# Block 0's attention with two groups of tokens in lockstep, and its weights loaded in two parts

## The chip, the cores and the metric

The kernel runs on one NeuronCore of a Trainium2 chip. Its engines are TensorE (PE: matmuls and transposes, with its own weight loads, PEld), VectorE (DVE), ScalarE (ACT), GpSimd (POOL) and SyncE (SP, which here only issues DMAs). Each engine runs its own instructions in the order in which they were written, and they meet at semaphores. The metric is the device time of one execution in microseconds (us); the figure is the median of several runs.

## The reference

A vision tower: a tokenizer (four Fourier layers) makes 8192 tokens of 64 features, and four blocks, each of an attention part and a feed-forward part, follow. The change touches the attention of block 0 alone. `x` below is the layer-normed `h`, taken as 128 sequences of 64 tokens:

```python
q = x @ Wq + bq
k = x @ Wk + bk
v = x @ Wv + bv
score = jnp.einsum('bnd,bmd->bnm', q, k) / jnp.asarray(d_a, q.dtype)
score = jax.nn.softmax(score, axis=2)
attn = jnp.einsum('bnm,bmd->bnd', score, v)
h = attn @ Wl + bl
mean = jnp.mean(h, axis=(0, 1))
var = jnp.mean((h - mean) ** 2, axis=(0, 1))
y = jax.nn.relu((h - mean) * jax.lax.rsqrt(var + BN_EPS) * gamma + beta)
return y + x
```

The mean and variance at its end run over all 8192 tokens, so that nothing of `y` can be computed before every token has been through the attention.

## The kernel before

The tokenizer (`build_tokenizer`) ends with all its tokens in DRAM, and a barrier. Then comes `build_blocks`. There SP issues the load of all weights (`wts`, 12765 columns of 128 partitions, fp32), of the constants (`cst`), and of the first tokens (`h`), in this order; the other engines wait for the first two on the semaphore `weights_loaded` (`loaded`, 32), and DVE also for the tokens (`h_in`).

The stage `l0a` follows: 8 passes (`ITERS`) over U = 2 units of 512 tokens each. Both units go through one set of tiles: `x_stacked` holds unit 0 and unit 1 side by side, so that one matmul with a block-diagonal weight serves both. One pass is one chain of steps, each on one engine and each waiting for the one before:

- DVE: statistics (L1517), aggregation (L1523), variance plus epsilon (L1541), centring (L1529); POOL: the power of -1/2 (L1547); DVE: scaling into `x_stacked` (L1535)
- PE: transposes, step `x.flip` (L1585); ACT copies them out as `xT_stacked` (L1596)
- PE: `q`, `k`, `v` (L1627; each fp32 matmul stands as two records); ACT evacuates `q` (L1718), DVE `k` (L1729) and `v` (L1731)
- PE: `scores`, 16 matmuls of 64x64; DVE: `max` (L1745) and `diff` (L1748) read them from PSUM; ACT: `exp` (L1720); DVE: sum (L1751), reciprocal (L1753) and product `p` (L1760), and beside the chain `hx` (L1783), which keeps the normed tokens
- PE: transposes `pT` (L1705), ACT copies them (L1722); PE: `attended`, 16 matmuls of 64x64; ACT copies them (L1724); PE: `hl`, a matmul of 512 columns for each unit; DVE: adds the bias into `hl` (L1786)

After pass i has made `hx` of a unit, SP loads that unit's next tokens into the same `h`. After the 8 passes DVE sums `hl` over all tokens (L2823), ACT squares it (L2803), and one long loop of 8 passes runs the stages `l0b` to `l3f`, which are not changed. The order on every engine is that of the code: `l0a_tensor`, `l0a_scalar`, `l0a_vector` and `ln_pool` are each the body of a loop. `need` is a wait on a step's count, and `done` or `done_both` count a step up. PSUM has 8 banks, `B[0][0..3]` and `B[1][0..3]`; a pass uses seven of them.

## Time and profile before

| | us |
|---|---|
| median of 3 runs (lowest to highest) | 8977.72 (8970.33 to 8978.99) |
| the profiled execution | 8975.14 |
| its span, first to last instruction | 8973.3 |
| in it: barrier's end to the first statistics of `l0a` | 21.7 |
| in it: the 8 passes of `l0a` | 209.1 |

The profile gives for each line and engine what was busy and when; "idle before" names what ended a wait. PE was busy for 81% of the span, DVE 64%, ACT 23%, POOL 2%. Those are averages over stages with different limits, so the part that the change touches is read from the timeline and from windows of it. The granted clock (PEclk) is the share of TensorE's full 2.4 GHz: 0.50 is 1.2 GHz.

### The profile page before, as it was taken

The page shows a single profiled execution, that of the slowest core. Times are in us where ns is not written, and L with a number is a line of the kernel's source. Part 1 is how long each engine was busy: PE and PEld are TensorE (multiplying, and loading weights), DVE is VectorE, ACT ScalarE, POOL GpSimd, SP SyncE. Part 2 cuts the span into 40 slices and gives each one's busy share as a digit, 9 for nine tenths or more (in the row PEclk, how much of TensorE's full clock was granted, in tenths as well). Part 3 has the DMA queues.
Part 4 walks back from the last instruction along what each step waited for, and adds up shares of the span by engine and source line. Part 5 has one row for each costly group of instructions (what it writes and reads, how often), then busy time and mean ns, then how long its engine had stood idle before and what let it go on. Part 6 is the DMA issues. An engine that isn't in the chain of part 4 may idle for free. (4 is left out here: it accounts for less than half of the span.)

```text
span 8973.3 us, 126646 instructions
## 1 busy us (share of the span) xinstructions
PE 7286.3 (81%) x40310; PEld 3633.7 (40%) x40310; DVE 5736.5 (64%) x11679; ACT 2020.7 (23%) x3374; POOL 208.5 (2%) x123
## 2 busy tenths in 40 slices
PE   6888886999999799999789999935666666666666
PEld 5544445444444544444442222223333333333333
DVE  4799995788887488888557777734445344454443
ACT  3221212111111211111222222212222322222222
POOL 0000000000000000000000000000000000000000
PEclk8999998999999799999899999957777878777778
DMA  7655557666666766666764444410000000000000
GB/s 216 136 123 122 126 125 205 181 179 179 179 181 176 217 180 179 179 179 179 191 180 117 123 119 120 111 45 1 2 1 2 1 2 2 1 2 2 1 2 2
DMA packets 641710, 957.43 MB, mean 107 GB/s; under 512 B 527640, under 2 KB 531296, under 8 KB 582758
## 3 DMA queue, kind: packets, MB, share of 16 engines
q1 hardware_dynamic: 641416, 953.52, 40.1%
q8 instruction: 183, 3.00, 0.1%
q14 instruction: 111, 0.91, 0.0%
HBM read 621.96 MB, written 344.28 MB: 108 GB/s over the span
## 5 line engine op out<-in xcount | busy, mean ns | idle before, releaser
L603 PE MATMUL abank<-inv_basis,mode_tile 128*128 128x512 f32 x2048 | 1019.5, 622 | 172.8 <-DMA mode_tile<-m_modes 164.0
L970 DVE TENSOR_TENSOR work<-inv_copy,abank 128x512 f32<-128x512 f32 x1024 | 657.4, 683 | 610.7 <-ACT inv_copy L845 610.2
L665 PEld LDWEIGHTS gbank<-fwd_basis,turned 128*128 128x128 f32 x6368 | 747.2, 193 | 369.7 <-issue 222.7
L665 PE MATMUL gbank<-fwd_basis,turned 128*128 128x128 f32 x6368 | 823.0, 283 | 51.3 <-ACT turned L853 51.3
L1001 DVE TENSOR_TENSOR arena<-zbank,work 128x512 f32<-128x512 f32 x1024 | 701.6, 685 | 208.0 <-PE zbank L638 207.9
L634 PE MATMUL zbank<-arena,conv_bd 128*64 128x512 f32 x3072 | 830.3, 619 | 3.0 <-DVE mixed L1159 2.2
L636 PE MATMUL zbank<-arena,conv_bd 128*64 128x504 f32 x3072 | 779.6, 586 | 0.0
L638 PE MATMUL zbank<-arena,conv_bd 128*64 128x504 f32 x3072 | 779.6, 586 | 0.0
L1003 DVE SCALAR_TENSOR_TENSOR arena<-arena 128x512 f32<-128x512 f32 x1024 | 708.5, 692 | 35.4
L853 ACT ACTIVATE turned<-tbank 128x512 f32<-128x512 f32 x796 | 432.0, 594 | 1100.7 <-PE tbank L652 1100.7
L603 PEld LDWEIGHTS abank<-inv_basis,mode_tile 128*128 128x128 f32 x2048 | 364.3, 196 | 540.1 <-issue 496.9
L652 PEld LDWEIGHTS tbank<-eye,work 128*128 128x128 f32 x3184 | 344.2, 141 | 367.8 <-issue 278.9
L652 PE MATMUL tbank<-eye,work 128*128 128x128 f32 x3184 | 437.6, 281 | 51.1 <-DVE work L1027 34.5
L845 ACT ACTIVATE inv_copy<-abank,conv_bias 128x512 f32<-128x512 f32 x256 | 176.0, 688 | 1237.5 <-PE abank L603 1237.5
L1585 PE MATMUL banks<-constants,x_stacked 128*128 128x128 f32 x256 | 69.5, 426 | 446.9 <-DVE x_stacked L1535 446.9
L802 PE MATMUL zbank<-mix_w,arena 128*128 128x128 f32 x1024 | 243.2, 414 | 208.1 <-DVE mix_w L1149 130.0
L1149 DVE SCALAR_TENSOR_TENSOR mix_w<-uv,twid,partial 128x512 f32<-128x512 f32 x256 | 181.1, 749 | 351.8 <-ACT partial L930 343.5
L636 PEld LDWEIGHTS zbank<-arena,conv_bd 128*64 128x64 f32 x3072 | 220.8, 137 | 440.2 <-issue 440.2
L638 PEld LDWEIGHTS zbank<-arena,conv_bd 128*64 128x64 f32 x3072 | 220.5, 137 | 428.4 <-issue 428.4
L845 ACT ACTIVATE inv_copy<-abank 128x512 f32<-128x512 f32 x256 | 152.9, 597 | 1060.1 <-PE abank L603 1060.1
L1627 PE MATMUL banks<-xT_stacked,weights 64*128 64x512 f32 (+1 forms) x912 | 347.3, 804 | 50.2 <-ACT xT_stacked L1596 37.9
L981 DVE TENSOR_TENSOR work<-work 128x512 f32<-128x512 f32 x512 | 352.3, 688 | 20.9
(306 smaller groups left out, 9251.8 us busy)
## 6 DMA issues: line engine op xcount, KB each, us to landing
h_rows<-arena SPq DMA_DIRECT2D x192, 1024.0 KB, 16.2
arena<-h_rows SPq DMA_DIRECT2D x192, 1024.0 KB, 6.1
arena<-h_rows SPq DMA_DIRECT2D x384, 496.0 KB, 8.7
m_modes<-mixed SPq DMA_DIRECT2D x64, 1024.0 KB, 6.7
mode_tile<-m_modes SPq DMA_DIRECT2D x512, 128.0 KB, 4.3
g_modes<-modes_out SPq DMA_DIRECT2D x192, 256.0 KB
arena<-x_slots SPq DMA_DIRECT2D x192, 194.9 KB
arena<-g_modes SPq DMA_DIRECT2D x36, 1024.0 KB, 10.8
```

Source lines behind the costliest of these rows:

```text
L603: last = nc.tensor.matmul(abank[px][:], mode_tile[u][:, 2 * px + k, :, :].rearrange("p a c -> p (a c)"), inv[:, 2 * px + k, :], start=True ...
L634: nc.tensor.matmul(out[a], conv_bd[:, 1, :], src[a], start=True, stop=False)
L636: nc.tensor.matmul(out[a][:, :, 1:COLS], conv_bd[:, 0, :], src[a][:, :, 0:COLS - 1], start=False, stop=False)
L638: last = nc.tensor.matmul(out[a][:, :, 0:COLS - 1], conv_bd[:, 2, :], src[a][:, :, 1:COLS], start=False, stop=True)
L652: last = nc.tensor.transpose(tbank[px][:, m:m + 128], folded[q][:, px, py, 128 * b:128 * b + 128], eye[:])
L665: last = nc.tensor.matmul(gbank[u][:, 128 * k:128 * k + 128], turned[q][:, k // 2, k % 2, b, :], fwd[:, 2 * q + b, k, :], start=(q == 0 an ...
L853: last = nc.scalar.activation(turned[q][:, px, :, :, :].rearrange("p y b n -> p (y b n)"), tbank[px][:], ACT.Identity)
L970: nc.vector.tensor_tensor(inverse[:, 2 * k + part, :], inv_copy[k][:], abank[1][:], op)\
L981: nc.vector.tensor_tensor(spectral[u][:, low, :, 0, :], base, delta, ALU.add)
L1001: nc.vector.tensor_tensor(out, zbank[o % 2][:], added, ALU.add).then_inc(z_full, 1)
L1003: nc.vector.scalar_tensor_tensor(out=out, in0=out, scalar=0.01, in1=out, op0=ALU.mult, op1=ALU.max)\
L1627: return nc.tensor.matmul(out, lhsT, rhs, start=start, stop=stop)
```

## The change

Four things are done. The 8 passes become 4, and a pass now carries two groups g of two units each: every step is written for group 0 and then for group 1, on every engine. Group 1 has tiles of its own, which the later stages use for other things (its `h` is `r`, its `x_stacked` and `xT_stacked` lie in `big`, its statistics in the new `small_b`). Group g keeps to the four banks `B[g][0..3]`, in which scores and attended reuse the banks of `flip` and `q`, and `hl` those of `pT` and `v`. And the weights come in two parts: constants first, then the 517 columns that block 0's attention needs, the tokens of the first pass, and behind these the other 12248 columns, on a semaphore of their own (`rest`), for which PE, ACT and DVE wait after the stage. The unused branch of `attn_vector`, which `l0a` alone had taken, is dropped.

```diff
- ('l0a', 'pe'): ['x.flip', 'q', 'k', 'v', 'scores', 'pT', 'attended', 'hl'],
+ ('l0a', 'pe'): IN_TWO(['flip', 'q', 'k', 'v', 'scores', 'pT', 'attended', 'hl']),
...
+        gh = pick(h, r)
+        gx = pick(x, sq)
+        g_q, g_k = pick(Q[0][:], K[1][:]), pick(K[0][:], H[0][:, 0, :])
+        g_st = pick(small, small_b)
...
-            stacked_tensor(p, "x", "x.out")
-            attn_tensor(p, "l0a")
-            p.need("act", "oT", 1)
-            for u in R:
-                p.done(mm(B[u][3][lo, :], W("l0a_l")[rows[u], :], a_oT[rows[u], :]), "hl", u)
+            for g in R:
+                for u in R:
+                    p.need("dve", f"x.out{g}", u)
+                for t in range(T):
+                    last = nc.tensor.transpose(B[g][0][:, 128 * t:128 * t + 128],
+                                               g_xs[g][:, t, :, :].rearrange("p u f -> p (u f)"), eye)
+                p.done_both(last)
+            for g in R:
+                p.need("act", f"xT{g}", 1)
+                p.done_both(mm(B[g][1][:], W("l0a_q"), g_xT[g]))
+            for g in R:
+                p.done_both(mm(B[g][2][:], W("l0a_k"), g_xT[g]))
+            for g in R:
+                for t in range(T):
+                    last = mm(B[g][3][:, 128 * t:128 * t + 128], g_xT[g][:, 128 * t:128 * t + 128], W("l0a_v"))
+                p.done_both(last)
+            for g in R:
+                p.need("act", f"q{g}", 1)
+                p.need("dve", f"k{g}", 1)
+                for b in range(BATCHES):
+                    for u in R:
+                        last = mm(B[g][u][rows[u], 64 * b:64 * b + 64], g_q[g][rows[u], 64 * b:64 * b + 64],
+                                  g_k[g][rows[u], 64 * b:64 * b + 64])
+                p.done_both(last)
+            for g in R:
+                p.need("dve", f"p{g}", 1)
+                for t in range(T):
+                    last = nc.tensor.transpose(B[g][2][:, 128 * t:128 * t + 128], g_e[g][:, 128 * t:128 * t + 128], eye)
+                p.done_both(last)
+            for g in R:
+                p.need("act", f"pT{g}", 1)
+                p.need("dve", f"v{g}", 1)
+                for t in range(T):
+                    for u in R:
+                        for n, part in HALVES:
+                            last = mm(B[g][n][rows[u], 64 * t:64 * t + 64], g_vv[g][part, t, u, :],
+                                      g_pT[g][part, t, 64 * u:64 * u + 64])
+                p.done_both(last)
+            for g in R:
+                p.need("act", f"oT{g}", 1)
+                for u in R:
+                    p.done(mm(B[g][2 + u][lo, :], W("l0a_l")[rows[u], :], g_o[g][rows[u], :]), f"hl{g}", u)
...
         def l0a_scalar(a):
-            stacked_scalar(a, "x")
-            attn_scalar(a, "l0a", 1.0 / 64)
+            for g in R:
+                a.need("pe", f"flip{g}", 1)
+                a.done_both(nc.scalar.activation(g_xT[g], B[g][0][:], ACT.Identity))
+            for g in R:
+                a.need("pe", f"q{g}", 1)
+                a.done_both(nc.scalar.activation(g_q[g], B[g][1][:], ACT.Identity, bias=W("l0a_bq")))
+            for g in R:
+                a.need("dve", f"diff{g}", 1)
+                a.done_both(nc.scalar.activation(g_e[g], g_e[g], ACT.Exp, scale=1.0 / 64))
...
+        def l0a_pool(p):
+            for g in R:
+                p.need("dve", f"x.vars{g}", 1)
+                p.done_both(nc.gpsimd.tensor_tensor(g_st[g][:, :, 8:12], g_st[g][:, :, 0:4],
+                                                    bmid(W("mhalf")[:, 0:4], U), ALU.pow))
         def l0a_vector(d):
-            def first(u):
-                d.eng.wait_ge(h_in[u], d.it * 16 + 16)
-            ln_vector(d, "x", h, x, first=first, out=x_of)
-            attn_vector(d, "l0a")
-            for u in R:
...
+            for g in R:
+                for u in R:
+                    d.eng.wait_ge(h_in[g][u], d.it * 16 + 16)
+                    for t in range(T):
+                        last = V.bn_stats(parts(g, u)[:, t, :], gh[g][u][:, t, :])
+                    d.done(last, f"x.stats{g}", u)
...
+            for g in R:
+                for u in R:
+                    d.need("pool", f"rstd{g}", 1)
+                    d.need("dve", f"x.centered{g}", u)
+                    d.done(V.tensor_tensor(g_xs[g][:, :, u, :], gx[g][u][:], bc(g_st[g][:, u, 8:12], 64), ALU.mult),
+                           f"x.out{g}", u)
+            for g in R:
+                d.need("pe", f"k{g}", 1)
+                d.done_both(V.tensor_scalar(g_k[g], B[g][2][:], W("l0a_bk"), None, ALU.add))
+            for g in R:
+                d.need("pe", f"v{g}", 1)
...
+            for g in R:
+                d.need("pe", f"scores{g}", 1)
+                for u in R:
+                    d.done(V.reduce_max(g_m[g][rows[u]], by_batch(B[g][u][rows[u], :]), axis=AX.X), f"max{g}", u)
+            for g in R:
+                d.need("dve", f"max{g}", 1)
+                for u in R:
+                    d.done(V.tensor_tensor(g_eb[g][rows[u]], by_batch(B[g][u][rows[u], :]), bc(g_m[g][rows[u]], SEQ),
+                                           ALU.subtract), f"diff{g}", u)
+            for g in R:
+                d.need("act", f"exp{g}", 1)
+                d.done_both(V.reduce_sum(g_s[g], g_eb[g], axis=AX.X))
+            for g in R:
+                d.need("dve", f"sum{g}", 1)
+                d.done_both(V.reciprocal(g_s[g], g_s[g]))
+            for g in R:
+                d.need("dve", f"recip{g}", 1)
+                d.done_both(V.tensor_tensor(g_eb[g], g_eb[g], bc(g_s[g], SEQ), ALU.mult))
+            for g in R:
+                for u in R:
+                    d.done(V.tensor_tensor(hx[:, bass.ds(T * token_block(d.it, g, u), T), :], gh[g][u][:],
+                                           g_xs[g][:, :, u, :], ALU.add), f"hx{g}", u)
+            for g in R:
+                for u in R:
+                    d.need("pe", f"hl{g}", u)
+                    d.done(V.tensor_scalar(hl[:, bass.ds(BLK * token_block(d.it, g, u), BLK)], B[g][2 + u][lo, :],
+                                           W("l0a_bl"), None, ALU.add), f"hl{g}", u)
...
+        first = where_w["l0a_beta"][1] + where_w["l0a_beta"][2]
-            sp.dma_start(wts[:], weights_dram).then_inc(loaded, 16)
             sp.dma_start(cst[:], consts_dram).then_inc(loaded, 16)
+            sp.dma_start(wts[:, 0:first], weights_dram[:, 0:first]).then_inc(loaded, 16)
...
-            for u in R:
-                sp.dma_start(h[u][:], tiles[u]).then_inc(h_in[u], 16)
-            with sp.Fori(1, ITERS) as it:
-                for u in R:
...
+            for g in R:
+                for u in R:
+                    sp.dma_start(gh[g][u][:], tiles[token_block(0, g, u)]).then_inc(h_in[g][u], 16)
+            sp.dma_start(wts[:, first:], weights_dram[:, first:]).then_inc(rest, 16)
+            with sp.Fori(1, ITERS // 2) as it:
+                for g in R:
+                    for u in R:
+                        sp.wait_ge(sig.sem("l0a", "dve"), sig.count("l0a", "dve", f"hx{g}", u, it) - sig.count("l0a", "dve", f"hx{g}", u, 1) + sig.count("l0a", "dve", f"hx{g}", u, 0))
+                        sp.wait_ge(ready, 1)
+                        sp.dma_start(gh[g][u][:], tiles[bass.ds(token_block(it, g, u), 1)].rearrange("b p t f -> (b p) t f"))\
+                            .then_inc(h_in[g][u], 16)
...
-            with pe.Fori(0, ITERS) as it:
+            with pe.Fori(0, ITERS // 2) as it:
                 l0a_tensor(Engine(sig, "pe", pe, "l0a", it, apart=True))
+            pe.wait_ge(rest, 16)
```

ACT, DVE and POOL get the same halved loop count, ACT and DVE the same wait for `rest` behind it.

PE, the body of the loop from the transposes to the scores, before:

```order
 L1585 MATMUL banks<-constants,x_stacked 128x128 x4
 L1443 ISA
 L1627 MATMUL banks<-xT_stacked,weights 128x512 x2
 L1627 MATMUL banks<-weights,xT_stacked 128x128 x4
 L1443 REGISTER_ALU x2
 L1627 MATMUL banks<-kt,qt 64x64 x16
```

and after (`big` stands for group 1's tiles; for the scores of group 1, `hid` and `kt`):

```order
598 L1784 MATMUL banks<-constants,x_stacked 128x128 x4
600 L1784 MATMUL banks<-constants,big 128x128 x4
602 L1631 MATMUL banks<-xT_stacked,weights 128x512
604 L1631 MATMUL banks<-big,weights 128x512
605 L1631 MATMUL banks<-xT_stacked,weights 128x512
606 L1631 MATMUL banks<-big,weights 128x512
607 L1631 MATMUL banks<-weights,xT_stacked 128x128 x4
608 L1631 MATMUL banks<-weights,big 128x128 x4
610 L1631 MATMUL banks<-kt,qt 64x64 x16
612 L1631 MATMUL banks<-hid,kt 64x64 x16
```

Group 1's instruction now stands between a step of group 0 and its next one, and `q` of group 0 stands behind the transposes of group 1.

DVE, from the maxima to the product, before:

```order
953 L1745 TENSOR_REDUCE small<-banks 64x8 x2
955 L1748 TENSOR_TENSOR big<-banks,small 64x512
957 L1748 TENSOR_TENSOR big<-banks,small 64x512
959 L1751 TENSOR_REDUCE small<-big 128x8
961 L1753 RECIPROCAL small<-small 128x8
963 L1760 TENSOR_TENSOR big<-big,small 128x512
```

and after:

```order
971 L1889 TENSOR_REDUCE small<-banks 64x8 x2
973 L1889 TENSOR_REDUCE small_b<-banks 64x8 x2
975 L1893 TENSOR_TENSOR big<-banks,small 64x512 x2
977 L1893 TENSOR_TENSOR big<-banks,small_b 64x512 x2
979 L1897 TENSOR_REDUCE small<-big 128x8
981 L1897 TENSOR_REDUCE small_b<-big 128x8
983 L1900 RECIPROCAL small<-small 128x8
985 L1900 RECIPROCAL small_b<-small_b 128x8
987 L1903 TENSOR_TENSOR big<-big,small 128x512
989 L1903 TENSOR_TENSOR big<-big,small_b 128x512
```

The sum of group 0, which waits for ACT's exponentials, now stands behind the `diff` of group 1.

## Rows read from the trace of the kernel before

**Rows 1.** Windows of the passes: engines' busy us, then PEclk, DMA share, GB/s.
```profile
5869.90:5896.80 26.90, 12.03 (x88) 7.07 (x88) 11.09 (x36) 3.11 (x5) 1.67 (x1) 0.56 0.05 11
5896.80:5922.10 25.30, 10.75 (x88) 6.14 (x88) 10.96 (x36) 3.11 (x5) 1.68 (x1) 0.63 0.05 10
...
sum 209.10, PE 92.23 PEld 53.48 DVE 88.35 ACT 24.86 POOL 13.40; mean PE 11.53 PEld 6.69 DVE 11.04 ACT 3.11 POOL 1.67
```

**Rows 2.** Timeline (start, us, engine, line) of the loads, and their window.
```profile
5848.20 0.35 SPq L2747 DMA_DIRECT2D weights<-in_weights  x1
5849.08 1.35 SPq L2752 DMA_DIRECT2D h<-tokens  x2
5869.94 1.11 DVE L1517 BATCH_NORM_STATS2 small<-h 128x6 f32<-128x64 f32 x8 [21.45 <-DMA h<-tokens]
...
5848.20:5869.90 21.70, 0.00 (x0) 0.00 (x0) 0.19 (x1) 0.00 (x0) 0.00 (x0) 0.50 0.94 376
```

**Rows 3.** Token loads in the passes: count, KB each, us to landing.
```profile
h<-tokens SPq DMA_DIRECT2D x14, 128.0 KB, 2.3
```

**Rows 4.** Timeline of the second pass, the chain's steps in order.
```profile
5896.77 1.09 DVE L1517 BATCH_NORM_STATS2 small<-h 128x6 f32<-128x64 f32 x8
...
5898.32 0.28 DVE L1541 TENSOR_SCALAR small<-small 128x4 f32<-128x4 f32 x2
...
5898.75 1.68 POOL L1547 TENSOR_TENSOR small<-small,constants 128x8 f32<-128x8 f32 x1 [25.14 <-DVE small L1541]
5900.55 0.76 DVE L1535 TENSOR_TENSOR x_stacked<-x,small 128x256 f32<-128x256 f32 x2 [1.28 <-POOL small L1547]
...
5903.38 3.43 PE L1627 MATMUL banks<-xT_stacked,weights 128*128 128x512 f32 x4 [0.84 <-ACT xT_stacked L1596]
...
5906.65 1.05 PE L1627 MATMUL banks<-weights,xT_stacked 128*128 128x128 f32 x8
...
5906.92 0.75 DVE L1729 TENSOR_SCALAR kt<-banks,weights 128x512 f32<-128x512 f32 x1 [5.61 <-PE banks L1627]
...
5907.82 1.15 PE L1627 MATMUL banks<-kt,qt 64*64 64x64 f32 x32
5909.00 1.41 DVE L1745 TENSOR_REDUCE small<-banks 64x8 f32<-64x512 f32 x2 [0.51 <-PE banks L1627]
...
5911.94 0.63 ACT L1720 ACTIVATE big<-big 128x512 f32<-128x512 f32 x1 [5.74 <-DVE big L1748]
...
5914.61 1.09 PE L1705 MATMUL banks<-constants,big 128*128 128x128 f32 x4 [5.64 <-DVE big L1760]
5915.79 0.60 ACT L1722 ACTIVATE pT<-banks 128x512 f32<-128x512 f32 x1 [3.22 <-PE banks L1705]
...
5916.73 1.13 PE L1627 MATMUL banks<-pT,big 64*64 64x64 f32 x32 [1.04 <-ACT pT L1722]
...
5918.72 1.97 PE L1627 MATMUL banks<-qt,weights 64*64 64x512 f32 x4 [0.86 <-ACT qt L1724]
5920.81 1.40 DVE L1786 TENSOR_SCALAR hl<-banks,weights 64x512 f32 x2 [5.68 <-PE banks L1627]
```

**Rows 5.** The same TensorE steps in the fourth pass, and windows of both passes.
```profile
5954.92 3.75 PE L1627 MATMUL banks<-xT_stacked,weights 128*128 128x512 f32 x4 [0.84 <-ACT xT_stacked L1596]
5958.46 1.92 PE L1627 MATMUL banks<-weights,xT_stacked 128*128 128x128 f32 x8
...
5907.50:5909.00 1.50, 1.35 (x34) 1.00 0.00 0
5957.50:5960.30 2.80, 2.80 (x10) 0.50 0.00 0
```

**Rows 6.** GpSimd's power in a later stage, with no vector instruction beside it.
```profile
6146.77 1.63 POOL L1547 TENSOR_TENSOR small<-small,constants 128x8 f32<-128x8 f32 x1 [35.49 <-DVE small L1566]
```

**Rows 7.** Instruction fetches by DMA in the eight passes: packets, MB.
```profile
q14 instruction: 2, 0.02, 0.0%
q8 instruction: 1, 0.02, 0.0%
```

More of the change, by code:

```diff
@@ L1362 @@
 TWICE = ['x.stats', 'x.aggr', 'x.vars', 'x.centered']
-STEPS = {('l0a', 'act'): ['x.xT', 'q', 'exp', 'pT', 'oT'],
- ('l0a', 'dve'): [*NORM('x'), 'k', 'v', 'max', 'diff', 'sum', 'recip', 'p', 'hx', 'hl'],
- ('l0a', 'pe'): ['x.flip', 'q', 'k', 'v', 'scores', 'pT', 'attended', 'hl'],
+IN_TWO = lambda names: [f'{s}{g}' for s in names for g in range(2)]
+STEPS = {('l0a', 'act'): IN_TWO(['xT', 'q', 'exp', 'pT', 'oT']),
+ ('l0a', 'dve'): IN_TWO(['x.stats', 'x.aggr', 'x.vars', 'x.centered', 'x.out', 'k', 'v', 'max', 'diff', 'sum', 'recip',
+                         'p', 'hx', 'hl']),
+ ('l0a', 'pe'): IN_TWO(['flip', 'q', 'k', 'v', 'scores', 'pT', 'attended', 'hl']),
  ('l0b', 'act'): ['y'],
@@ L1484, in build_blocks @@
         loaded = sem("weights_loaded")
-        h_in = [sem(f"h_loaded{u}") for u in R]
+        h_in = [[sem(f"h_loaded{g}_{u}") for u in R] for g in R]
+        rest = sem("other_weights_loaded")
         out_sent = [sem(f"out_sent{u}") for u in R]
@@ L1764, in blk @@
             return U * it + u
[L1766 to L1787 removed]
+        pick = lambda a, b: (a, b)
@@ L2770, in _ @@
             pool.wait_ge(loaded, 32)
-            with pool.Fori(0, ITERS) as it:
-                ln_pool(Engine(sig, "pool", pool, "l0a", it), "x")
+            with pool.Fori(0, ITERS // 2) as it:
+                l0a_pool(Engine(sig, "pool", pool, "l0a", it))
             pool.wait_ge(bn_done["dve"], 4)
@@ L2798, in _ @@
             act.wait_ge(loaded, 32)
-            with act.Fori(0, ITERS) as it:
+            with act.Fori(0, ITERS // 2) as it:
                 l0a_scalar(Engine(sig, "act", act, "l0a", it))
+            act.wait_ge(rest, 16)
             act.wait_ge(bn_done["dve"], 2)
@@ L2814, in _ @@
             dve.wait_ge(loaded, 32)
-            with dve.Fori(0, ITERS) as it:
+            with dve.Fori(0, ITERS // 2) as it:
                 l0a_vector(Engine(sig, "dve", dve, "l0a", it))
+            dve.wait_ge(rest, 16)
             done = bn_done["dve"]
```

73 lines of the change are left out of this document (48 added, 25 removed).

## The prediction, made before the changed kernel was run

> **What bounds the kernel now.** The page of the whole span says TensorE, busy 81%, but this change touches one stretch near the middle, so I read that stretch alone, first in windows and then in the timeline. The windows of the eight passes add up to 209.1 us, in which TensorE is busy for 92.2 and VectorE for 88.4 [rows 1]. Neither is near full: the stretch is bound by latency. The timeline shows why. Within a pass each instruction starts about 0.1 us after the end of the one before it on another engine, and nothing else is queued [rows 4]: VectorE idles 5.61 us until k is there, TensorE 5.64 us until the softmax is done. A pass of 25.3 to 26.9 us [rows 1] is the sum of the steps. Ahead of the passes stands a second serial piece: the weights are issued at 5848.20, the tokens behind them, and the first statistics run at 5869.94, released by the tokens' DMA, after 21.7 us at 376 GB/s with TensorE idle [rows 2]. All tokens must pass before the batch statistics, so nothing behind hides either piece: a microsecond taken from them is taken from the end.
>
> **The load.** In the old order 6382.5 KB of weights, 1324 KB of constants (2648 columns of 128 partitions, 4 bytes each) and two tiles of 128 KB go ahead of the first statistics: 8.15 MB in 21.74 us. In the new order the constants (1.356 MB), 517 columns (0.265 MB) and two token tiles (0.262 MB) do: 1.88 MB. A token tile alone lands 2.3 us after its issue [rows 3], of which I take 2.0 as fixed. Then 8.15 MB went at 413 GB/s, and 1.88 MB needs 2.0 + 4.6 = 6.6 us: 15.1 us saved. If nothing were fixed, 1.88 MB at 376 GB/s is 5.0 us, 16.7 saved. If each of the two small tiles cost a fixed 1 us more, 13 saved. I take 15, since the tile of 128 KB is the only small transfer the trace shows. SP's issues (1.35 us for two [rows 2]) run beside the transfer. Group 1's tokens follow within about 1 us, when DVE is still at group 0's statistics. The other 6.27 MB need about 17 us more behind them and are awaited only after the stage, 140 us later, so that cost is nothing; were that cover gone, it would be those 17 us.
>
> By the Trainium skill (DMA: Bandwidth & Descriptors, section Bandwidth, its measured table) a transfer of 1 MB runs at 341 GB/s, well under what a long one reaches. By that figure the load would take 2.0 + 5.5 = 7.5 us, an estimate that costs 0.9 us of the gain; the trace has only the long train at 376, so it doesn't decide.
>
> **The passes.** Nothing is removed. Two chains of the same steps run staggered by one step, so a step costs the longer of its latency and two turns on its engine. I lay out one new pass from its first statistics, with durations of [rows 4].
>
> - *Head.* From statistics to variance an old pass takes 1.55 us (5896.77 to 5898.32); the new one does this for both groups, with group 0's variance 1.55 later, so GpSimd starts at 1.98 + 1.55 = 3.5. Its two powers run back to back, 2 x 1.68, to 6.9. Group 1's scaling follows at 7.0 to 7.8, its transposes start at 7.9. These take 0.9 us of TensorE's queue, and q of group 0, though its input is ready at 8.2, stands behind them: q starts at 8.8, where it started at 6.6 before (5903.38).
> - *q, k, v and scores.* Eight long fp32 passes (512 columns), 16 short ones, two sets of scores. At the half clock a long one takes 0.87 us (3.54 us from the first to the first v in the fourth pass, four of them [rows 5]), at full clock half of it. The clock rises inside this block: in the second pass it is 1.00 about 4 us after q's start and k ended early (3.43 us against 3.75), in the fourth it is still 0.50 at 5.4 us [rows 5]. So I place the rise between 2.8 and 5.4 us after q's start. The v passes then cost 1.05 per group (1.92 cold [rows 4, 5]), scores 1.05 of issue. Group 0's scores end 8.2 us after q's start with the early rise, 9.4 with the late one, 11.7 if the clock never rose. VectorE's four evacuations of 0.75 or less fit beside it. The maxima start 0.2 later, at 17.2 to 18.4 (cold 20.7); I take 17.9.
> - *Maxima to product.* From the maxima to the exponentials an old pass takes 2.94 us; for two groups VectorE needs 2 x 2.8 = 5.6. The exponentials of group 0 (0.63) lie beside group 1's differences; those of group 1 are waited for. From there to the transposes of group 0 the old chain takes 2.67 us (5911.94 to 5914.61), and so does the new one: at 26.2. `hx` stays beside it.
> - *Tail.* From transposes to the next statistics an old pass takes 5920.81 - 5914.61 + 1.4 = 7.6 us. Attended (1.13), the copies (0.60) and the transposes of group 1 fill gaps of group 0. The last matmuls do not: `hl` of two units takes 1.97, about 1.7 of it issue, and group 1's stands behind group 0's. So 9.3, and the pass ends at 35.5.
>
> The bounds: 34.7 with the early rise, 36.0 with the late one, and 34.0 if the clock also rises under `hl`. Two old passes took 209.1/4 = 52.3. Four new ones take 142 against 209.1: 67 saved, 61 to 73 over the bounds with 0.5 us a pass for waits I have not seen. VectorE, at 22 us of 35.5, is still not the bound.
>
> Added waits: SP waits for `hx` of each group in turn; it follows the product, at 27 to 28 of a pass, about 8 us before the next pass's statistics of that group, against a landing of 2.3 us [rows 3], so it hides. On GpSimd nothing is queued behind its two powers.
>
> GpSimd's second power now runs beside the scaling of group 0, a vector instruction with two inputs in SBUF. In the old passes it ran beside the centring, which is of the same kind, and took 1.68 us; alone it takes 1.63 [rows 4, 6]. So 0.05 us. The Trainium skill (Advanced Engine Details and Errata, section GPSIMD Details) says that Pool and DVE share a read and a write interface and that an instruction with two SBUF inputs conflicts. Were they to take turns fully, 0.8 us a pass would be added, 3 us in all; the trace speaks against it.
>
> **Sum.** 15 + 67 = 82 us off the profiled 8975.1: 8893. The median of the runs is 2.6 us above the profiled execution, so 8895 to 8896; I say 8895.
>
> **Rivals.**
> - *The clock stays low.* If the gaps of a new pass keep TensorE at 0.50 throughout, a pass is 38.3 us, the four 153, and with a load gain of 15 the sum is 71: 8906. Against it: a new pass has denser matmuls than an old one, and in both old kinds of pass it rose by the scores (mean 0.56 and 0.63 [rows 1]).
> - *The tokens don't get ahead of the rest.* If their small packets are served in turn with the big load, the stage starts only when all is in, and only the 67 us remain: 8911. Against it: the tokens, issued last, came last before, so the queue looks ordered; but nothing in the trace is issued behind them.
> - *The stagger doesn't work.* If engines reach the groups' steps so that each waits for the other group, for example VectorE queued before group 1's differences while TensorE needs group 0's sum, a pass would be some 45 us instead of 35.5: 38 us less gain, 8933.
> - *Slower.* The loop's body has doubled. The eight old passes fetched three packets of instructions [rows 7], so the body stays at hand. If the doubled one has to be fetched anew in every pass, and the engines stand until it comes, each pass loses that time. It decides against the change from (82 + 18)/4 = 25 us a pass; at 27 us the kernel is at 9003. The only sign for it is the doubling itself.
> - *Better.* Clock high early and under `hl`, load at its best: 73 + 17 = 90, 8888.
>
> **How the numbers follow.** The forecast (8888 to 8902) 0.68; the low clock or small new waits (8902 to 8910) 0.15; tokens not ahead 0.06; better than 8888 0.04; the stagger fails 0.04, of which 0.01 comes within 0.2% of the old time; slower 0.02; something of no effect 0.01. 0.2% is 18 us, about what a measurement of this kernel can tell from no change. Faster 0.96, same 0.02, slower 0.02. The range takes in forecast, low clock and the late tokens, with the 4 us by which runs scatter: 8884 to 8914.
>
> **What would show it.** Right: first statistics about 6.6 us after SP's first issue; starts of the passes 35 to 36 us apart; TensorE's q of group 0 right behind group 1's transposes; VectorE without a gap from maxima to group 1's differences; the passes over about 149 us after SP's first issue, where it was 21.7 + 209.1 = 231, and the later stages as long as before. Wrong: a pass over 38 us, idle time of VectorE released by a token DMA inside the passes, a start of the stage near 20 us after the issue, or a later stage that has changed length.

## The result and the profile after

The changed kernel takes 8904.15 us (median of 4 runs, 8898.74 to 8906.37) against 8975.75 (4 runs, 8970.33 to 8978.99) for the one before on the same chip: ratio 0.992, 95% interval 0.9903 to 0.9937, 71.6 us faster. The prediction said 8895 and 8884 to 8914. The profiled execution took 8904.87, with a span of 8903.1 against 8973.3: 70.2 us, so the two traces can be set against each other.

I cut both traces at the same three events: SP's first issue of a load, the first statistics, and the sum over `hl` that follows the first stage (us).

| stretch | before | after | gain |
|---|---|---|---|
| start to SP's first issue (code untouched) | 5848.20 | 5854.34 | -6.1 |
| first issue to first statistics | 21.74 | 6.95 | 14.8 |
| the passes of the first stage | 209.12 | 136.62 | 72.5 |
| everything after them | 2894.24 | 2905.19 | -10.9 |
| sum | 8973.3 | 8903.1 | 70.2 |

So the edited stretch gave 87.3 us, 5 more than forecast. 17 were lost in code that nobody touched. The experiments below are about these.

**The load.** The first rows of the timeline (start, us, engine, line, names; in brackets the idle time before and its releaser), and the window of the load, answer to [rows 2]:

```profile
5854.34 0.35 SPq L2873 DMA_DIRECT2D constants<-in_constants  x1
5854.75 0.42 SPq L2874 DMA_DIRECT2D weights<-in_weights  x1
5855.22 1.32 SPq L2879 DMA_DIRECT2D h<-tokens  x2
5856.58 1.62 SPq L2879 DMA_DIRECT2D r<-tokens  x2
5858.24 2.27 SPq L2880 DMA_DIRECT2D weights<-in_weights  x1
5861.29 0.83 DVE L1855 BATCH_NORM_STATS2 small<-h 128x6 f32<-128x64 f32 x5 [6.66 <-DMA h<-tokens]
...
5854.30:5861.20 6.90, 0.00 (x0) 0.00 (x0) 0.19 (x1) 0.00 (x0) 0.00 (x0) 0.50 0.89 283
```

The statistics wait for `h` alone. The rest of the weights is issued at 5858.24, three microseconds before the tokens are used, and does not hold them up.

**The passes.** The windows of the four passes (busy us of PE, PEld, DVE, ACT, POOL, then the granted clock, DMA share, GB/s), which answer to [rows 1]:

```profile
5861.30:5895.50 34.20, 16.45 (x176) 11.19 (x176) 21.84 (x71) 6.22 (x10) 4.42 (x2) 0.71 0.54 205
5895.50:5929.50 34.00, 16.56 (x176) 11.26 (x176) 21.55 (x71) 6.22 (x10) 4.42 (x2) 0.75 0.07 15
...
sum 136.60, PE 66.28 PEld 45.00 DVE 86.70 ACT 24.86 POOL 17.69; mean PE 16.57 PEld 11.25 DVE 21.67 ACT 6.22 POOL 4.42
```

Three things are to be seen. VectorE is busy for 86.7 us in all, against 88.4: the same work in two thirds of the time. TensorE's busy time fell from 92.2 to 66.3 with the same matmuls: the mean granted clock, 0.56 and 0.63 in the two old windows, is 0.71 and 0.75 in these. GpSimd's rose from 13.4 to 17.7, though it does the same eight powers.

The second pass step by step (timeline), which answers to [rows 4]:

```profile
5895.47 1.09 DVE L1855 BATCH_NORM_STATS2 small<-h 128x6 f32<-128x64 f32 x8
...
5898.82 0.74 DVE L1870 TENSOR_TENSOR x<-h,small 128x256 f32<-128x256 f32 x2
5898.91 2.82 POOL L1845 TENSOR_TENSOR small<-small,constants 128x8 f32<-128x8 f32 x1 [29.54 <-DVE small_b L1867]
5899.49 0.74 DVE L1870 TENSOR_TENSOR sq<-r,small_b 128x256 f32<-128x256 f32 x2
5901.70 1.63 POOL L1845 TENSOR_TENSOR small_b<-small_b,constants 128x8 f32<-128x8 f32 x1
5901.85 0.76 DVE L1876 TENSOR_TENSOR x_stacked<-x,small 128x256 f32<-128x256 f32 x2 [1.62 <-POOL small L1845]
...
5903.45 0.76 DVE L1876 TENSOR_TENSOR big<-sq,small_b 128x256 f32<-128x256 f32 x2 [0.84 <-POOL small_b L1845]
...
5904.36 1.09 PE L1784 MATMUL banks<-constants,big 128*128 128x128 f32 x4 [0.52 <-DVE big L1876]
...
5905.24 1.92 PE L1631 MATMUL banks<-xT_stacked,weights 128*128 128x512 f32 x2
...
5908.43 1.02 PE L1631 MATMUL banks<-xT_stacked,weights 128*128 128x512 f32 x2
...
5913.22 1.41 DVE L1889 TENSOR_REDUCE small<-banks 64x8 f32<-64x512 f32 x2 [0.33 <-PE banks L1631]
...
5917.54 1.41 DVE L1893 TENSOR_TENSOR big<-banks,small_b 64x512 f32<-64x512 f32 x2
...
5921.57 1.94 PE L1807 MATMUL banks<-constants,big 128*128 128x128 f32 x8 [7.46 <-DVE big L1903]
...
5925.68 1.08 PE L1631 MATMUL banks<-qt,weights 64*64 64x512 f32 x4
5926.56 1.05 PE L1631 MATMUL banks<-hid,weights 64*64 64x512 f32 x4
5926.88 2.72 DVE L1911 TENSOR_SCALAR hl<-banks,weights 64x512 f32 x4 [3.51 <-PE banks L1631]
5929.52 1.09 DVE L1855 BATCH_NORM_STATS2 small<-h 128x6 f32<-128x64 f32 x8
```

The interleaving shows in the pairs: the centring of `h` and of `r`, q of `xT_stacked` and then of `big`, `hl` of `qt` and of `hid`. q's two matmuls at 5905.24 take 1.92 us (half clock), k's at 5908.43 take 1.02 (full clock). The two groups of `hl` take 1.08 and 1.05 us, where two units took 1.97 in the old pass. The windows of these matmuls, before and then after, show a granted clock of 0.50 and of 1.00 (the third number from the end):

```profile
5918.80:5920.80 2.00, 1.89 (x4) 0.21 (x4) 0.00 (x0) 0.00 (x0) 0.00 (x0) 0.50 0.00 0
```

```profile
5926.00:5929.00 3.00, 1.62 (x8) 0.33 (x4) 2.12 (x4) 0.27 (x1) 0.00 (x0) 1.00 0.15 34
```

### The profile page after: what moved, and what is told of

Read it like the earlier page. It is cut to its first block and busy times, and to the rows that moved or that the text cites. A ratio compares the mean times of both kernels' runs of the same rounds, so it can differ in the third digit from the quotient of the medians.

```text
span 8903.1 us, 126581 instructions
## 1 busy us (share of the span) xinstructions
PE 7282.2 (82%) x40310; PEld 3629.5 (41%) x40310; DVE 5737.0 (64%) x11679; ACT 2020.2 (23%) x3374; POOL 212.8 (2%) x123
## 5 line engine op out<-in xcount | busy, mean ns | idle before, releaser
L981 DVE TENSOR_TENSOR work<-work 128x512 f32<-128x512 f32 x512 | 352.4, 688 | 20.9
```

The lines of the kernel that those rows point to most:

```text
L981: nc.vector.tensor_tensor(spectral[u][:, low, :, 0, :], base, delta, ALU.add)
```

## The experiments

The kernels were run in three groups of four, each beside the kernel before (medians 8976.31, 8975.64 and 8973.67). "Later" is the time from the sum over `hl` to the end in the profiled execution. "Long passes" are the times of the loop's passes in the later stages, from one first power of the loop to the next. "Fetches" are packets of the instruction queue q14 per such pass. Load, passes, later, long passes and fetches come from one profiled execution of each kernel; the median and the ratio come from all its runs.

| kernel | load | passes | later | long passes | fetches | median | ratio (95%) |
|---|---|---|---|---|---|---|---|
| before | 21.74 | 209.12 | 2894.2 | 360.7, then 358.0-358.6 | 9 | 8975.75 | |
| after | 6.95 | 136.62 | 2905.2 | 358.6-361.6 | 15 | 8904.15 | 0.9920 (0.9903-0.9937) |
| e1, new load alone | 7.19 | 209.09 | 2891.8 | 358.1-358.8 | 9 | 8962.35 | 0.9985 (0.9976-0.9995) |
| e2, new passes alone | 21.68 | 136.11 | 2898.8 | 357.4-362.8 | 15 | 8907.04 | 0.9924 (0.9907-0.9940) |
| e3, before + 16, 62, 194 | 26.34 | 221.26 | 2901.1 | 357.6-362.5 | 15 | 9002.34 | 1.0032 (1.0020-1.0043) |
| e4, after + 112, 66, 62 | 11.58 | 137.15 | 2890.2 | 356.5-358.7 | 9 | 8892.62 | 0.9908 (0.9891-0.9924) |
| e6, after + 112 | 6.97 | 136.44 | 2912.1 | 358.9-362.3 | 10 | 8909.15 | 0.9923 (0.9906-0.9939) |
| e7, e6 and late centring | 7.07 | 134.55 | 2909.5 | 357.1-362.5 | 10 | 8906.34 | 0.9923 (0.9907-0.9940) |
| e8, before, longer power | 21.32 | 208.56 | 2892.1 | 357.9-359.0 | 9 | 8973.74 | 0.9999 (0.9989-1.0009) |
| e9, before + 16 on ScalarE | 21.69 | 208.89 | 2890.6 | 357.3-358.6 | 14 | 8976.35 | 1.0001 (0.9991-1.0010) |
| e10, before + 62 on VectorE | 21.81 | 209.09 | 2900.4 | 356.9-361.4 | 10 | 8976.62 | 1.0004 (0.9994-1.0013) |
| e11, before + 194 on TensorE | 22.54 | 210.28 | 2885.8 | 352.4, then 358.3-358.5 | 9 | 8973.90 | 1.0002 (0.9993-1.0012) |
| e12, after + 66 on VectorE | 7.06 | 137.06 | 2892.1 | 358.3-358.6 | 14 | 8886.74 | 0.9906 (0.9889-0.9922) |
| e13, after, all shifts, late centring | 7.24 | 134.57 | 2892.2 | 358.0-358.9 | 9 | 8884.90 | 0.9903 (0.9886-0.9920) |

### One part alone: e1 and e2

The new order of the loads in the kernel before:

```diff
-            sp.dma_start(wts[:], weights_dram).then_inc(loaded, 16)
             sp.dma_start(cst[:], consts_dram).then_inc(loaded, 16)
+            sp.dma_start(wts[:, 0:first], weights_dram[:, 0:first]).then_inc(loaded, 16)
...
                 sp.dma_start(h[u][:], tiles[u]).then_inc(h_in[u], 16)
+            sp.dma_start(wts[:, first:], weights_dram[:, first:]).then_inc(rest, 16)
```

with a wait for `rest` on PE, ACT and DVE behind the first stage.

> The eight old passes, but the weights in two parts and in the new order. Theory of the sum: from SP's first issue to the first statistics 7 us instead of 21.7, the passes 209 as before, so 14.8 us faster than before if the later stages keep their 2894 us. Rival (the later stages lengthen whenever code is moved or the load is split): 7 and 209 as well, but later stages of about 2905, so only 4 us faster.

Measured: 8962.35, 14.0 us faster, first statistics 7.19 us after the first issue, passes and later stages as before. Part alone and part in the sum agree (14.0 and 14.8).

The changed kernel with all weights in front again:

```diff
+            sp.dma_start(wts[:], weights_dram).then_inc(loaded, 16)
             sp.dma_start(cst[:], consts_dram).then_inc(loaded, 16)
-            sp.dma_start(wts[:, 0:first], weights_dram[:, 0:first]).then_inc(loaded, 16)
...
-            sp.dma_start(wts[:, first:], weights_dram[:, first:]).then_inc(rest, 16)
```

> The four new passes, but all the weights loaded ahead as before. Theory of the sum: 21.7 us to the first statistics, passes of 136.6 us together (34.2 each, 72.5 us less than before). Later stages 2894 if the 11 us that the changed kernel spends more in them come from the split load, 2905 if they come from the new passes (their code or the moment at which they end). Total 72 us or 62 us faster than before.

Measured: 8907.04, 69.3 us faster, though the four passes took 136.11 us, 73.0 less than before. The load took 21.68 again. The passes do not depend on the load, so the local gains add up: 14.5 and 73.0 make 87.5, where the changed kernel shows 87.3. The totals do not: 14.0 and 69.3 make 83, where the changed kernel is 71.6 faster. Between this kernel's median and the changed one's (8907.04 and 8904.15) the new load, worth 14.0 in e1, is worth 2.9 us. The later stages are long here too, 2898.8 us, with 15 fetches a pass, without any change to the loads. So what lengthens them comes with the new passes. That they took 6.4 us less here than in the changed kernel's profile accounts for about half of the missing 12; the rest is not explained. One more row of this kernel's timeline shows what SP would have paid had it issued more behind the full load: its queue took the third and fourth token tile only after 16 us.

```profile
5855.44 1.29 SPq L2878 DMA_DIRECT2D h<-tokens  x2
5856.77 16.16 SPq L2878 DMA_DIRECT2D r<-tokens  x2
```

### Where the code lies: e3 and e4

The later stages execute the same instructions in both kernels, yet fetch more of them. The view of the DMA queues, over the later stages alone (packets, MB, share), gives for before (6079 to 8973)

```profile
q14 instruction: 73, 0.60, 0.1%
```

and for after (5998 to 8903)

```profile
q14 instruction: 117, 0.96, 0.1%
```

The new first stage has more instructions in each engine's stream ahead of the long loop: 16 on ScalarE, 62 on VectorE, 194 on TensorE. **Theory:** this moves the loop's code, more of it is fetched anew in each pass, and some fetches are waited for. **Rival:** the place of the code is of no account, and the later stages end later by chance, or because they start at another point of the clock's rhythm. e3 puts as many instructions into the kernel before (waits that are already met, each carried by an empty instruction; the trace counts the pair as one). e4 fills the changed kernel up so that the loop lies a multiple of 128 instructions from its old place: 16 + 112, 62 + 66, 194 + 62.

```diff
             dve.wait_ge(loaded, 32)
+            for _ in range(62):
+                dve.wait_ge(loaded, 32)
+                dve.nop(nofuse=True)
```

and in the same way 16 on ScalarE and 194 on TensorE (e3); 66, 112 and 62 in the changed kernel (e4).

> The kernel before with waits that are already met put ahead of the first stage, 16 on ScalarE, 62 on VectorE, 194 on TensorE, so that the code of the long loop lies where it lies in the changed kernel. Theory that the place of the code lengthens the later stages: instruction fetches on q14 in a pass of the long loop rise from 9 to 15, and the later stages take about 2905 us instead of 2894. Rival (the rhythm of TensorE's clock against the passes, or scatter between executions): fetches may rise, but the later stages stay at 2894, or change without regard to them. The first stage costs at most 3 us more.

> The changed kernel with such waits, 112 on ScalarE, 66 on VectorE, 62 on TensorE, so that the long loop's code lies as in the kernel before by blocks of 128 instructions. Theory of the place of the code: fetches on q14 fall back to 9 a pass and the later stages to 2894, so about 9 us faster than the changed kernel (the added waits cost 1 to 2 of the 11 in the first stage). Rival (clock rhythm or scatter): later stages of 2905 whatever the fetches do.

Measured, e3: fetches rose from 9 to 15 a pass, as in the changed kernel, and the later stages to 2901.1 us. The total of +26 us is mostly the padding itself, which is dearer than I had thought: VectorE's 62 waits delayed the first statistics by 4.6 us, and TensorE's 194 held its first transposes, ready at 5885.1, until 5897.28, which is 12.2 us.

```profile
5884.30 0.76 DVE L1535 TENSOR_TENSOR x_stacked<-x,small 128x256 f32<-128x256 f32 x2 [1.27 <-POOL small L1547]
5897.25 0.72 PEld L1585 LDWEIGHTS banks<-constants,x_stacked 128*128 128x128 f32 x4 [49.41 <-issue]
```

Measured, e4: fetches back to 9, later stages 2890.2, and the kernel at 8892.62, 11.5 us under the changed one, although its 66 waits on VectorE cost 4.6 us of load (11.58 for 6.95). The two together bear the theory out: the old kernel's later stages got longer when their code was moved, and the new one's got shorter. But the padding also ended the first stage at another time, 16.7 us later in e3 and 5.2 in e4, so these two alone do not rule out the clock's rhythm. e12 below does, as its first stage takes within 0.6 us what the changed kernel's does.

### Which engine: e6, e9, e10, e11, e12

Five kernels move one engine's code at a time. From e10 on the padding stands ahead of the wait for the load, on a semaphore set early, so that it runs while the data come: the edit is `wait_ge(ready, 1)` in place of `wait_ge(loaded, 32)`.

**ScalarE.** e6 moves it in the changed kernel by 112, e9 in the old one by 16:

```diff
             act.wait_ge(loaded, 32)
+            for _ in range(16):
+                act.wait_ge(loaded, 32)
+                act.nop(nofuse=True)
```

> The changed kernel with 112 met waits ahead of the first stage on ScalarE alone, 128 instructions with the 16 that the change adds there. Theory that ScalarE's code is the one that counts: fetches on q14 in a pass of the long loop 9 instead of 15, later stages 2890 us, the load 6.95 us again (the 4.6 us that the waits on VectorE cost are gone), so about 4 us below the kernel with all three engines realigned: 8888 to 8890. Rival (VectorE's or TensorE's code counts): fetches stay at 15 and the time near 8904.

> The kernel before with 16 met waits ahead of the first stage on ScalarE alone, behind which nothing waits. Theory that the place of ScalarE's code lengthens the later stages: q14 15 fetches a pass, later stages 2899 to 2905 us instead of 2894, 6 to 11 us slower than the kernel before; the load and the eight passes unchanged. Rival: 9 fetches and the same time as before.

Measured: this place sets five of the six additional fetches (15 to 10 in e6, 9 to 14 in e9) and costs nothing that shows. e9 takes 8976.35 against 8975.64 (the interval reaches from 8 us less to 9 more) with later stages of 2890.6. e6 takes 8909.15, so nothing came back, and the later stages were the longest of all. The view of the waits, over the later stages, shows where the cost of the fetches went (what waited, on what: us in total, times, longest; "issue" is a wait for nothing that the profile shows). First ScalarE in e9, then VectorE in the kernel before:

```profile
ACT L1793 <- issue: 20.3, 7, 3.1
```

```profile
DVE qt L1805 <- issue: 17.0, 7, 2.6
```

ScalarE, which has no such row in the kernel before, waits once in each of the loop's seven returns to its start, where VectorE has such a wait anyway. So the number of fetched packets is a sign that code was moved, not a price.

**VectorE and TensorE**, in the kernel before (62 and 194), and VectorE in the changed one (66):

```diff
             nc.vector.memset(gs[:], 0.0).then_inc(ready, 1)
+            for _ in range(66):
+                dve.wait_ge(ready, 1)
+                dve.nop(nofuse=True)
             dve.wait_ge(loaded, 32)
```

> The kernel before with 62 met waits on VectorE alone, ahead of its wait for the weights, where it stands idle for 21 us. Theory that VectorE's code is the one that counts: one more fetch a pass on q14 (10 for 9), passes of the long loop of 361 among those of 358, later stages 2899 to 2912 us instead of 2894, so 7 to 15 us slower than the kernel before. Rival (TensorE's code counts): as before within 3 us.

> The kernel before with 194 met waits on TensorE alone, ahead of its wait for the weights; they take some 14 us of the 21 in which it is idle. Theory that VectorE's code counts: as before within 3 us, passes of 358.4. Rival (TensorE's code counts): passes of 361 among them, 7 to 15 us slower.

> The changed kernel with 66 met waits on VectorE alone, so that its part of the long loop lies as before, put into the 7 us in which it waits for the weights. Theory that VectorE's code counts: q14 14 fetches a pass (those of ScalarE stay), all passes 358.4, later stages 2890 to 2894, the first stage as in the changed kernel (7.0 and 136.6): 8888 to 8892. Rival (TensorE's): 8904 as the changed kernel.

Measured: e12, 8886.74 us (8885.45 to 8892.33), 17.4 under the changed kernel and 15.3 under it when each is taken against its own runs of before. All its runs lie under all of the changed kernel's. Its later stages are back at 2892.1, with the long passes at 358.3 to 358.6, and this with 14 fetches a pass: of the changed kernel's 15 the one that counts is VectorE's. TensorE's place costs nothing that shows: e11 has 9 fetches, 8973.90 us against 8973.67 and no longer later stage, and e12 leaves TensorE's and ScalarE's code moved. The other instruction queue, q8, has 18 packets in a pass of the long loop in before, after, e9, e11 and e12 alike.

e10 is less clear. Its profiled execution has the signs of the changed kernel (10 fetches, passes up to 361.4, later stages 2900.4), but that run, 8984.43, is one of two high ones among ten. The other eight lie between 8974.8 and 8978.7, the median is 2.9 us over before, and the interval (0.9994 to 1.0013, from 5 us less to 12 more) holds no difference as well as the expected one. So the cost of VectorE's place is shown on the changed kernel, and not on the old one, where it seems to come in some executions only.

Over all fourteen profiles, one of each kernel, the two kinds do not overlap. With VectorE's code moved (after, e2, e3, e6, e7, e10) the later stages take 2898.8 to 2912.1 us. With it in its old place, or a multiple of 128 from it, (before, e1, e4, e8, e9, e11, e12, e13) they take 2885.8 to 2894.2. The gap between the kinds is only 4.6 us, but the single passes say the same more clearly. Of the seven intervals from pass to pass, leave out the first, which scatters (352 to 362 us): two to four of the other six are over 361 us in each kernel of the first kind, and none of the 48 in the second kind is over 359.0. VectorE's code was tried at three places only (0, 62 and 128 instructions along), so which other places are good, and whether 128 is the period, is not shown.

### A wait of 0.2 us, and passes of 361 us

In the view of the waits, from the second long pass on (engine, what waited, on what: us in total, times, longest), the changed kernel's VectorE has a row that e12's has not:

```profile
DVE small L1527 <- issue: 1.3, 7, 0.2
DVE qt L1930 <- issue: 15.2, 6, 2.7
```

e12 has only one row of VectorE with "issue":

```profile
DVE qt L1930 <- issue: 14.6, 6, 2.5
```

The row of 0.2 us stands in the profiles of all six kernels with VectorE's code moved (in e2 for two passes only), and in none of the other eight. The 0.2 us a pass stand in the normalisation ahead of the loop's first power, and behind the same power the scaling is slower. The timeline of the changed kernel has 1.00 us for it:

```profile
6388.92 1.00 DVE L1539 TENSOR_TENSOR r<-sq,small 128x256 f32<-128x256 f32 x2 [2.52 <-POOL small L1562]
6389.84 0.75 DVE L1539 TENSOR_TENSOR x<-sq,small 128x256 f32<-128x256 f32 x2
```

and that of e12 has 0.76 for the same pair:

```profile
6384.32 0.76 DVE L1539 TENSOR_TENSOR r<-sq,small 128x256 f32<-128x256 f32 x2 [2.52 <-POOL small L1562]
6385.00 0.75 DVE L1539 TENSOR_TENSOR x<-sq,small 128x256 f32<-128x256 f32 x2
```

In e10, the old kernel with VectorE's code moved, the gap is seen between the two instructions of such a pair: they start at 6471.40 and 6471.97 and take 0.42 us each. That is 0.4 us a pass directly, 3 us in the eight passes, against 10.9 measured (13.1 against e12). The rest comes in passes of about 361 us among those of 358.6. A long one (361.6) and a shorter one (358.7) follow each other in the changed kernel. The timeline of TensorE in the long one:

```profile
6609.85 1.09 PE L1589 MATMUL banks<-constants,x_stacked 128*128 128x128 f32 x4 [5.39 <-DVE x_stacked L1539]
6611.96 3.78 PE L1631 MATMUL banks<-xT_stacked,weights 64*128 64x512 f32 x8 [1.02 <-ACT xT_stacked L1600]
6615.67 3.16 PE L1631 MATMUL banks<-hid,weights 128*64 128x512 f32 x8
```

and at the same place of the next:

```profile
6971.64 1.09 PE L1589 MATMUL banks<-constants,x_stacked 128*128 128x128 f32 x4 [5.37 <-DVE x_stacked L1539]
6973.74 3.37 PE L1631 MATMUL banks<-xT_stacked,weights 64*128 64x512 f32 x8 [1.02 <-ACT xT_stacked L1600]
6977.23 1.08 PE L1631 MATMUL banks<-hid,weights 128*64 128x512 f32 x4
6978.55 1.08 PE L1631 MATMUL banks<-hid,weights 128*64 128x512 f32 x4 [0.23 <-ACT hid L2453]
```

and the windows of the `hid` matmuls (length, TensorE busy, granted clock):

```profile
6615.70:6618.90 3.20, 3.13 (x10) 0.61 0.00 0
6977.20:6979.60 2.40, 2.13 (x8) 1.00 0.00 0
```

The same sixteen matmuls end 6.9 us after their start in the first pass and 5.9 in the second, because the granted clock rises about 3 us later. In the next stage the ten `xT_stacked` matmuls take 5.77 us in the long pass and 4.63 in the other. These two places make up 2.1 of the 2.9 us between the two passes. That a few tenths lost early in a pass shift the clock's rise, and so cost some microseconds later in it, is my reading and not shown: the 0.2 us are lost in the short passes too, and the rows show only that the late rise comes in the long ones. **A test whether any such delay does it** is e8: the kernel before, with the last stage's power over 5 columns in place of 4 (the fifth result is thrown away), which takes 1.99 us in place of 1.67:

```diff
+                p.done_both(nc.gpsimd.tensor_tensor(small[:, :, 8:13], small[:, :, 0:5], bmid(W("mhalf")[:, 0:5], U),
+                                                    ALU.pow))
```

> The kernel before with GpSimd's power in the last stage of the long loop taken over 5 columns instead of 4 (one column is thrown away), which makes it some 0.3 us longer in each of the 8 passes and leaves all code in its place. Theory that the passes follow the rhythm of TensorE's clock: the time does not grow by 8 x 0.3 = 2.5 us; the passes stay at 358.4 us as long as the rise of the clock takes the delay up, or fall into the changed kernel's alternation of 358.8 and 361.3, 8 to 12 us more. Rival (no such rhythm; the alternation comes from the fetches): all passes 358.7 to 358.8, 2.5 us more in all.

Measured: 8973.74 against 8975.64, ratio 0.9999 (0.9989 to 1.0009), passes of 357.9 to 359.0. Eight times 0.32 are 2.6 us, less than the medians can tell; the traces say more. From the second long pass on the mean is 358.39 us in e8 and 358.44 before, so 0.3 us a pass at this place vanish. The passes keep to about 358.4 over this delay, at this place and in this one profile, while the one on VectorE goes with passes of 361. Why 62 instructions on VectorE do so and the power does not, which instruction's fetch is awaited, and how the rhythm locks, stays open.

### GpSimd beside the centring: e7 and e13

In the changed kernel group 0's power takes 2.82 us, beside four centring instructions of VectorE. In the old pass, with two beside it, it took 1.68 [rows 4], alone 1.63 [rows 6]. Theory: the centring holds GpSimd up. Rival: the power is slow there for another reason, such as its wait on two groups' variances. The edit centres group 1 only when group 0 has been scaled:

```diff
- ('l0a', 'dve'): IN_TWO(['x.stats', 'x.aggr', 'x.vars', 'x.centered', 'x.out', 'k', 'v', ...
+ ('l0a', 'dve'): IN_TWO(['x.stats', 'x.aggr', 'x.vars']) + ['x.centered0', 'x.out0', 'x.centered1', 'x.out1'] + ...
```

> The kernel with ScalarE realigned, and VectorE centres group 1 only after it has scaled group 0. Theory that four centring instructions beside GpSimd's first power slow it from 1.68 to 2.81 us: the first power takes 1.7 us again, and a pass is shorter by up to 1.1 us, 4 us in all, against the same kernel without this. Rival (the power is as long because of something else, or the slowing only moves to the second power, beside which the centring then lies): a first power of 2.8, or a second one above 2.5, and passes as long as before within 1 us in all.

> All three engines realigned, with the waits inside the wait for the weights, and group 1 centred after group 0's scaling. Both theories: load 7.0, passes 134.6, later stages 2890, so 4.6 us (the waits now hidden) and 2 us (the shorter power) below the first realigned kernel: 8886 to 8888, the fastest of all. Rival (the later stages fall into the slower rhythm by the shorter first stage too): 8895 or more.

Measured, in the timeline of GpSimd in e7:

```profile
5894.29 2.15 POOL L1845 TENSOR_TENSOR small<-small,constants 128x8 f32<-128x8 f32 x1 [29.95 <-DVE small_b L1867]
5896.41 1.64 POOL L1845 TENSOR_TENSOR small_b<-small_b,constants 128x8 f32<-128x8 f32 x1
```

The first power gives back 0.67 of its 1.14 us, and a pass becomes 0.5 us shorter: the four take 134.55 against 136.44 (e6), and 134.57 against 137.06 (e12, e13). Only the order of the centring was changed, so the theory holds for 0.67 of the 1.14 us. It is not the whole: 2.15 is still 0.47 over the old pass's 1.68, also with two centring instructions beside it, and that difference is open. The one thing that the traces show to differ is that the centring began 0.24 us before the power in the old pass and 0.09 before it here.

In the medians e7 gains 2.8 us over e6, with overlapping runs. e13, which has all shifts ahead of the wait for the load and the late centring, is the fastest kernel: 8884.90 (8882.83 to 8887.34), 88.8 us under before. Over e12 that is 1.8 us, again with overlapping runs; the traces alone show its 2.5 us in the stage.

## Why the prediction came out as it did

The time lies inside the range, 9 us above the forecast; of the 82 us forecast, 71.6 came. It fell in the band of 8902 to 8910, which the prediction gave 0.15 and put down to a low clock or small new waits. That is not what happened: the clock was higher than laid out, one new wait of 1 us a pass was more than paid for by it, and the excess came from the later stages. Step by step:

- **Load: right.** 6.95 us from issue to statistics where 6.6 was said, 14.8 saved for 15.1. The estimate of 7.5 by the Trainium skill's table (DMA: Bandwidth & Descriptors, section Bandwidth) is as near: the six kernels with the new load and no padding behind VectorE's wait for it show 6.95 to 7.24, between the two. The rival that small tokens are served in turn with the big load is refuted: they came in 7 us with 6.3 MB behind them.
- **The head: 1 us short.** The first power starts 3.44 us into the second pass, as laid out (3.5), but the second ends at 7.9 for 6.9, scaling of group 1 starts at 8.0 for 7.0, and q at 9.8 for 8.8. The step that failed is the sentence "the trace speaks against it". I looked at the power beside the scaling, where nothing happened (1.63), and took two centring instructions, worth 0.05, for the price of four. The measured price is 1.14. The rule of the Trainium skill (Advanced Engine Details and Errata, section GPSIMD Details), that vector instructions with two SBUF inputs conflict with Pool, fits the power beside the centring (1.14 us longer, 0.67 of which e7 took back) and did not show beside the scaling, which also has two inputs there and for which the prediction had worked out its 0.8 us a pass.
- **q to scores: 1.1 us too long.** q's start to the maxima took 8.0 us where I placed 9.1 and gave 8.4 as the early bound. The clock was up 3.0 us after q's start, near the early end of the 2.8 to 5.4 laid out. The two misses cancel, and the maxima start 17.75 us into the pass (17.9 said).
- **Maxima to transposes: right.** VectorE has no gap from the maxima to group 1's differences, and the transposes start at 26.1 (26.2 said).
- **The tail: 1.35 us too long.** It took 7.95 for 9.3. The full clock stayed under `hl`, so its two groups take 1.08 and 1.05 us and not 1.97 each. I had this case, with 34.0 a pass, as the bound below, and took the 1.97 of the old pass, where the windows show 0.50. The passes take 34.15 us, not 35.5, and the stage gave 72.5 us, not 67. (One sum on the way is off: passes of 36.0 us with 0.5 for waits leave 63 us saved at the least, not 61, and 3.54 us for four matmuls are 0.885 each, not 0.87. Nothing hangs on either.)
- **"The later stages as long as before": wrong,** and by more than all the rest. They became 10.9 us longer. A later stage that has changed length stood among its own signs of being wrong. The prediction did look at fetched instructions [rows 7], but only in the first stage, for its doubled body, as the rival on the other side. There nothing happened: the four passes fetched two packets of each queue. The cost arose in the loop behind, whose code was pushed along by an amount which `STEPS` and the diff do not show and which counts of instructions do. e12 took 15.3 us of it back by 66 instructions that do nothing.
- **The start: not foreseen, and not explained.** The tokenizer ended 6.1 us later in this one profile. Over the fourteen profiles SP's first issue lies between 5845.5 and 5856.9 us, with no order by kernel, so I take it for scatter of the execution. It is in the difference of the two spans; the medians contain it only in part.

So the mechanism of the two edited pieces was right, and their size nearly so. That the sum came within 9 us is in part luck: 5 us more than forecast in these pieces stand against a loss of 11 behind them that I had put at nothing.

## What to carry to other kernels

When a change lengthens the code ahead of a long loop, compare the loop behind it too: its instruction fetches per pass, and the short "issue" waits on the engine that sets its pace. If they rise, try the same kernel with a few dozen idle instructions ahead of the loop, placed where the engine waits anyway. Here 66 on VectorE gave 15 us. When two groups share one queue, price the case in which the closer matmuls are also granted the full clock: here it was the bound of the forecast, and it came. When two engines work side by side, price the overlap from a row with the same number of instructions beside it, and keep the instructions with two SBUF inputs out of GpSimd's time where nothing needs them yet.

## What the runs showed of the hardware

- The place of a loop's code has a price that differs by engine. VectorE moved by 62 instructions: one fetch a pass more, and 15 us in the medians of the changed kernel (e12 against it), which the old kernel's medians do not show (e10, 2.9 us more, not clear of zero). ScalarE moved by 16: five fetches more, 0.7 us in the medians (e9). TensorE moved by 194: no fetch more, 0.2 us (e11).
- A long loop can hold its time over a small delay (0.3 us a pass in e8 cost nothing that shows), and single passes of the same code can be 2.5 us longer when TensorE's clock rises at a later matmul.
- A wait that is already met is not free. 62 of them with their empty instructions cost VectorE 4.6 us, some 74 ns each. On TensorE 194 took 21.1 us (e3, e11), some 109 ns each, of which 12.2 held its first transposes up in e3. On ScalarE 112 took 6.4 us (e4, e6), 57 ns each.
- GpSimd's power of 128 x 8 took 1.63 us alone, 1.67 to 1.68 in the old passes beside two centring instructions, 2.15 beside two in e7 and e13, 2.82 beside four, and 1.63 beside two scaling instructions.
